# Setting the pad rows of the expert queues in nine stages during the front, in place of pads at the front's end

## The reference

```
x = layernorm(x + dilated_attention(x))           # 16 heads, segments of 64, every second token
x = layernorm(x + cross_attention(x, ctx))        # 16 heads, causal, keys and values from ctx
x = layernorm(x + moe(x))
# moe: probs = softmax(x @ gate_w); 8 of 32 experts for each token, weights renormalised
#      pairs are sorted by expert; an expert takes at most C = 1024 of them (2048*8/32*2), the rest are dropped
#      y = (silu(xg @ w_gate) * (xg @ w_up)) @ w_down ;  out[token] += weight * y
```

## Time and profile before

| | us |
|---|---|
| median of 3 runs | 622.81 (622.03 to 623.3) |
| the profiled execution | 623.45 |
| its span, first to last instruction | 621.8 |
| PE busy | 512.0 (82%) |
| DVE busy | 367.2 (59%) |
| ACT busy | 335.4 (54%) |
| POOL busy | 399.8 (64%) |

### The profile page before, as it was taken

How to read it: one execution, slowest core, us unless ns; L and a number is a source line. 1 busy time by engine, 2 the same in 40 slices (tenths; PEclk the granted TensorE clock), 3 DMA queues, 4 the chain that set the end, 5 groups by cost and what they waited for, 6 DMA issues and landing times.

```text
span 621.8 us, 17381 instructions
## 1 busy us (share of the span) xinstructions
PE 512.0 (82%) x5065; PEld 393.7 (63%) x5066; DVE 367.2 (59%) x1527; ACT 335.4 (54%) x1204; POOL 399.8 (64%) x604
## 2 busy tenths in 40 slices
PE   2888998888888888885119999999999999994994
PEld 2555555555555555542008888888888888883773
DVE  1468787777777787763304555555555555552664
ACT  2266666666666666663005666666666666661112
POOL 6553666666666666556715777777777768774653
PEclk9599999999999999996558999999999999996998
DMA  9999999932222222222785656656655556666994
GB/s 196 281 242 311 343 341 338 337 135 84 74 74 84 74 79 80 77 85 90 260 272 164 183 177 180 185 171 189 188 180 176 179 171 186 186 180 249 427 418 153
DMA packets 82301, 121.30 MB, mean 195 GB/s; under 512 B 13011, under 2 KB 71901, under 8 KB 80224
## 3 DMA queue, kind: packets, MB, share of 16 engines
q1 hardware_dynamic: 64896, 79.51, 42.0%
q0 software_dynamic: 14016, 38.44, 17.4%
q10 hardware_dynamic: 3360, 2.98, 1.5%
HBM read 56.07 MB, written 69.01 MB: 201 GB/s over the span
## 4 chain that ended last, share of the span: by engine, by line
PE 42%; POOL 16%; issue 14%; DVE 12%; DMA 6%; ACT 5%; ACTq 3%; POOLq 1%; SPq 1%; DVEq 0%
PE bank L796 16%; PE bank L812 11%; POOL queues L533 10%; PE bank L788 7%; DMA wall<-results 4%; DVE kP L1048 3%; ACT pr L873 3%; PE bank L806 3%; ACTq L297 2%; POOL rz L498 1%; POOL rz L492 1%; POOL pair_z L569 1%; DVE nmax L1025 1%; PE bank L614 1%; PE bank L604 1%
## 5 line engine op out<-in xcount | busy, mean ns | idle before, releaser
L559 POOL DMA_INDIRECT results<-ys,wcol x152 | 150.2, 988 | 26.2 <-POOL pscrap L548 24.1
L533 POOL DMA_INDIRECT queues<-x,xidx x128 | 128.5, 1004 | 37.2 <-issue 36.3
L796 PE MATMUL bank<-wall,xtT 128*128 x616 | 127.0, 329 | 0.1
L873 ACT ACTIVATE pr<-bank,nmax 128x128 f32<-128x128 f32 x256 | 90.9, 370 | 29.1 <-DVE nmax L1025 29.1
L796 PEld LDWEIGHTS bank<-wall,xtT 128*128 128x128 f32 x616 | 98.5, 194 | 0.5 <-issue 0.5
L966 ACT ACTIVATE ys<-bank,wcol 128x256 f32<-128x256 f32 x152 | 72.1, 474 | 44.5 <-PE bank L812 44.5
L1219 DVE SCALAR_TENSOR_TENSOR tg<-th,bank 128x96 f32<-128x96 f32 x154 | 39.1, 254 | 90.8 <-ACT th L960 90.6
L788 PE MATMUL bank<-ident,xt 128*128 128x128 f32 x310 | 63.4, 286 | 34.2 <-DMA xt<-queues 22.9
L812 PE MATMUL bank<-wall,hT 96*128 x304 | 90.8, 380 | 0.0
L788 PEld LDWEIGHTS bank<-ident,xt 128*128 128x128 f32 x310 | 59.2, 198 | 48.7 <-DMA xt<-queues 23.9
L604 PE MATMUL bank<-kP,qS 128*128 128x512 f32 x128 | 67.1, 606 | 0.0
(11 more groups left out here) (178 smaller groups left out, 879.6 us busy)
## 6 DMA issues: line engine op xcount, KB each, us to landing
xt<-queues SPq DMA_DIRECT2D x162, 160.0 KB, 2.2
results<-zeros SPq DMA_DIRECT2D x16, 1024.0 KB
wall<-results SPq DMA_DIRECT2D x16, 1024.0 KB, 13.9
queues<-zeros SPq DMA_DIRECT2D x32, 160.0 KB, 2.8
wall<-in_L_ffn_w_gate SPq DMA_DIRECT2D x4, 768.0 KB, 11.5
wall<-in_L_ffn_w_up SPq DMA_DIRECT2D x4, 768.0 KB, 13.6
wall<-in_L_ffn_w_down SPq DMA_DIRECT2D x4, 768.0 KB, 13.0
results<-ys,wcol POOLq DMA_INDIRECT x152, 2.6
```

Of the source, the lines that this page charges most:

```text
L533: pool.indirect_dma_start(xg, bass.IndirectOffsetOnAxis(ap=xidx[:, par, k:k + 1], axis=0), x2[:, par, :], None, bounds_check=last_row, oob ...
L559: pool.indirect_dma_start(yr, bass.IndirectOffsetOnAxis(ap=wcol[:, u, 1:2], axis=0), ys[:, u, :], None, bounds_check=last_y, oob_is_err=Fa ...
L796: ins = pe.matmul(bank[2 + u % 2][:, 0:2 * INTER].rearrange("p (g i) -> p g i", g=2), xtT[:, u % 2, kk, :], wall[:, bass.ds(e, GU)].rearrange(
L873: ins = act.activation(pr[:, g % 2, q, :], pS[g % 2][:, q * P:(q + 1) * P], ACT.Exp, bias=nmax[:, 4 * g + q:4 * g + q + 1], accum_out=den[ ...
```

## The change

SP no longer sets results right after the weight loads. It works through 16 stages, one DMA each, and waits for each before the next (semaphore `cleared`). Stage s, for s from 0 to 8 (QT is 8), sets rows s*128 to s*128+127 of all 32 queues to the pad row, in one DMA of 128 x 32 rows. Stages 9 to 15 each set one 1 MB block of `results` (blocks 0 to 6). Then come the 18 idle blocks and the other nine blocks of `results` (7 to 15, semaphore `yr_zero`), with no waits between them. POOL waits in the front for stage r ahead of tile r's copy and scatters. The pads at the front's end go with their waits on SP, ACT and POOL, and with them `tab_p`, `eoff` (one copy on POOL) and the matmul that counted for `tab_p`.

```diff
-        def pad_queues(eng, engine, first, last, signal):
-            for e0 in range(first, last, 8):
-                rows = neighbours(engine, tab_p[0:1, e0:min(e0 + 8, last)], NE * STRIDE - P)
-                for r in rows:
-                    eng.dma_start(xg[bass.ds(r, P), :], zeros[:, :]).then_inc(signal, 16)
...
             sp.wait_ge(consts, N_CONST)
+            queues_v = xg[0:NE * STRIDE, :].rearrange("(e s p) w -> s p e w", e=NE, p=P)
+
+            def clear_results(b, signal):
+
+                r = b * P * TOPK
+                sp.dma_start(yr[r:r + P * TOPK, :].rearrange("(p k) d -> p k d", k=TOPK),
+                             zeros[:, 0:D].unsqueeze(1).to_broadcast([P, TOPK, D])).then_inc(signal, 16)
+
+            for s in range(NB):
+                if s <= QT:
+                    sp.dma_start(queues_v[s], zeros[:, :].unsqueeze(1).to_broadcast([P, NE, XW])).then_inc(cleared, 16)
+                else:
+                    clear_results(s - QT - 1, cleared)
+                sp.wait_ge(cleared, 16 * (s + 1))
             for k in range(IDLE):
                 r = NE * STRIDE + k * P
                 sp.dma_start(xg[r:r + P, :], zeros[:, :]).then_inc(idle_zero, 16)
-            for b in range(NB):
...
-            sp.wait_ge(dveH.sem, dveH.at(0, "tp"))
-            pad_queues(sp, ET.SP, 0, PADS[0], pad_zero)
+            for b in range(NB - QT - 1, NB):
+                clear_results(b, yr_zero)
+
             sp.wait_ge(dveH.sem, dveH.at(0, "tx"))
...
             for k in range(2):
                 sp.wait_ge(scattered[k], 16 * TOPK * NB // 2)
-            sp.wait_ge(pad_zero, 16 * PADS[1])
-            sp.wait_ge(pad_late, 16 * (NE - PADS[1]))
             sp.wait_ge(idle_zero, 16 * IDLE)
...
-                put(pool.tensor_copy, eoff[:, :], eoff_i[:, :])
...
                     pool.wait_ge(dveR.sem, dveR.at(r, "idx"))
+                    pool.wait_ge(cleared, 16 * (r + 1))
                     if not last:
                         keep(r, par)
...
             three_stages(pool, step, lambda: None)
 
-            pool.wait_ge(dveH.sem, dveH.at(0, "tp"))
-            pad_queues(pool, ET.Pool, PADS[1], NE, pad_late)
             keep(NB - 1, (NB - 1) % 2)
...
             pool.wait_ge(dveH.sem, dveH.at(0, "tx"))
-            pool.wait_ge(yr_zero, 16 * NB)
+            pool.wait_ge(yr_zero, 16 * (QT + 1))
...
                 pe.wait_ge(actB.sem, actB.at(NB - 1, "T3"))
-                pe.matmul(pW[0:1, 96:96 + NE], onesb[:, 0:1], seen[:, :], start=True, stop=True)
...
-            act.wait_ge(dveH.sem, dveH.at(0, "tp"))
-            pad_queues(act, ET.Activation, PADS[0], PADS[1], pad_zero)
...
-                dve.tensor_tensor(tab_p[0:1, :], pW[0:1, 96:96 + NE], eoff[0:1, :], ALU.add).then_inc(s, 1)
```

More of the change, by code:

```diff
@@ L37 @@
 YB = 10
-PADS = (14, 28)
 LAST = (4, 4, 4, 2, 2)
@@ L46 @@
 B_CONST = FIRST_CONST + 23
-N_CONST = 54
+N_CONST = 53
 assert MAXB % UN == 0
@@ L118, in build @@
         eoff_i = sb("eoff_i", [P, NE], I32)
-        eoff = sb("eoff", [P, NE])
         ufar = sb("ufar", [P, NE])
@@ L192, in build @@
         tab_x = sb("tab_x", [1, TAB + 2 * LEAD], I32)
-        tab_p = sb("tab_p", [1, NE], I32)
         tab_n = sb("tab_n", [1, 1], I32)
@@ L237, in build @@
         peH = Steps(sem("peH"), "count place table")
-        dveH = Steps(sem("dveH"), "took tp nblk nblkb skipb cum past n n2 fe fx tg tw tx")
+        dveH = Steps(sem("dveH"), "took nblk nblkb skipb cum past n n2 fe fx tg tw tx")
         peF = {n: sem(f"peF_{n}") for n in ("xT", "gu", "hT", "y")}
@@ L252, in build @@
         idle_zero = sem("idle_zero")
-        pad_zero = sem("pad_zero")
-        pad_late = sem("pad_late")
+        cleared = sem("cleared")
         yr_zero = sem("yr_zero")
@@ L331, in _ @@
                 sp.dma_start(xg[r:r + P, :], zeros[:, :]).then_inc(idle_zero, 16)
-            for b in range(NB):
-                r = b * P * TOPK
-                sp.dma_start(yr[r:r + P * TOPK, :].rearrange("(p k) d -> p k d", k=TOPK),
-                             zeros[:, 0:D].unsqueeze(1).to_broadcast([P, TOPK, D])).then_inc(yr_zero, 16)
-            sp.wait_ge(dveH.sem, dveH.at(0, "tp"))
-            pad_queues(sp, ET.SP, 0, PADS[0], pad_zero)
+            for b in range(NB - QT - 1, NB):
+                clear_results(b, yr_zero)
             sp.wait_ge(dveH.sem, dveH.at(0, "tx"))
```

## The result

| | before | changed |
|---|---|---|
| median of the runs, us | 622.54 (4 runs, 622.03 to 623.3) | 654.45 (4 runs, 653.46 to 657.74) |
| ratio | | 1.0507 (95% interval 1.0475 to 1.0539) |
| the profiled execution | 623.45 | 653.46 |
| its span | 621.8 | 651.7 |

A forecast was written before the change was run, and what follows sets the result against it. The loop through POOL was taken to bound the front, with zeroing stages pacing it after the change. 623.45 + 44 lateness - 9.9 pads = 657.5, less 0.6 is 656.9, taken as 656; range 640 to 680.

The forecast's parts named there:

- The loop through POOL: Front: next tile's reciprocal root stands behind this tile's scatters on POOL, so holding POOL holds the front; step 16.5 us.
- What goes, 9.9 us: Front's end: without pads, first block load follows the last scatter's landing, 9.9 us sooner; bounds 9 to 10.5.
- Start of stage 0, end at 68.2: SP's first stage: issued at 47.72 behind weight loads, done at 68.2; front 8.6 us late at its first scatter.
- Period 20.9: Stages 1 to 8: 19.05 us of bytes at 344 GB/s plus the dry gap, against 16.5; tile 8 44 us late.
- After stage 8: Stages 9 to 15 take 5.9 us each; remaining zeros end near 325, hidden before the last scatter at 353; lateness stays 44.
- The clock, cost nothing: PE in stages 0 to 8: clock falls to 0.50 in stalls, hidden by the stage; costed at nothing, 16 us without cover.
- B: Rival, full rate: stages stream like 8 KB rows, period 17.2, +2.4 us, 625, including everything up to 638; chance 0.10.
- C: Rival, faster: clears keep up with the front, period 15.4, only stage 0's 6.7 us remain, 619.6; chance 0.04.
- the rule of the Trainium skill: Stage with scatters: 2.0 us + bytes/436 GB/s per DMA gives 17.0 us, change near level; weighed against 344 GB/s from the trace.
- D: Rival, slow writes: rows spread over 32 queues write slower; 718 at 253 GB/s, 682 at 300; chance 0.10.
- E: Rival, clock: PE at 0.50 for most of each step makes the loop 23.3 us, 19 us more, 675; chance 0.06.

The follow-up runs named there:

- run with eight stages and both orders: Changed kernel with stages and seven results blocks ahead of expert weights, two stages in flight, stage 8 replaced by a results block: 612.17 us, ratio 0.9812 against the kernel before.

## Why the prediction was right

*The loop through POOL.* Right: nine tiles in a row wait for the stages, the rest of the front follows them, and its own step behind the gate is still 16.4 to 16.5. The run with eight stages and both orders shows that taking the gate's lateness away gives all of it back.

*What goes, 9.9 us.* Measured 10.1 in the profile and 9.8 (ratios 1.0664 and 1.0507) when the pads were kept. The last scatter landed 2.5 after its start, and the first block load went 2.7 after it, 2.9 forecast; the 2.6 borrowed from the results' scatters was good.

*Start of stage 0, end at 68.2.* Measured 68.3. SP issued it at 46.64, not 47.72, and the rate for zeros alone came out at 376, not 369.

*Period 20.9.* Measured (231.38 - 68.36)/8 = 20.4. The two parts were each a little too high: 18.7 to 18.8 for the bytes (350 GB/s; 19.05 at 344 forecast) and 1.5 for the drain (1.9 forecast), by the run with two stages in flight. Over eight stages this is the 4 us by which the lateness, 44 forecast, was 39.8. It is nearly all the error of the sum in this profile: 657.5 by the sum, 653.5 measured. The prediction allowed up to 0.5 us a stage for scatters that move in the dry gap, 4 in all, and took 0.9; the whole allowance would have met the profile. Whether the drain is short for that reason no run tells apart.

*After stage 8.* The cover held, with more to spare: SP was through with issuing at 303.5, the first block load at 351. Stages 9 to 15 took 4.8 each, not 5.9. What the prediction did not see is that traffic which ends late went with a loss of 2.9 and 4.6 us at the front's last scatters before it was itself the last thing waited for; in the changed kernel it ended early enough, in two of the experiments not.

*The clock, cost nothing.* Right for the changed kernel: the granted clock was 0.87 on average from 66 to 231, and the period stayed the stage's. But the cover is the gate. In the profile of the run with the pads kept the low clock reached into the first free step, and that step was 2.4 us longer. The changed kernel's runs spread over 4.3 us, those of before over 1.3; that this is where the spread comes from is only argued.

*The rivals.* B and C asked for a stage to go at the rate of 8 KB rows. It went at 350. By the rule of the Trainium skill weighed in the prediction (DMA: Bandwidth & Descriptors, section Anatomy of one DMA — SWDGE (gpsimd) path), which is stated for DMAs of GpSimd's path, a stage is estimated at 17.0. Applied to SP's stages, the trace agrees with neither its slope for these rows (350 GB/s) nor, quite, its fixed part, 2.0 there and a drain of 1.5 here. D asked for slow writes to 32 queues: 376 GB/s says no. E asked for POOL to wait for VectorE, with a loop of 23.3. In the changed kernel it waited for the zeros at all nine tiles, and with two stages in flight the front kept a period of 18.8, so the loop itself takes no longer than that.

## What to carry to other kernels

A wait put into a loop costs (its supply's period less the loop's own) for every turn that it gates, so compare the two periods first: bytes over the rate of the nearest rows of the same size, with all that shares the engines, plus the drain if each transfer is waited for alone. Before giving up on such a change, look at what stands ahead of the supply in its queue and at how many are in flight: here the order of one queue and a second semaphore turned +32 us into -10 (ratio 0.9842), and with one stage fewer into -12. And free DMA time is only free where it ends ahead of the next burst of small transfers that someone waits for.

## What the runs showed of the hardware that was not expected

- Rows of 1280 B written to 32 places 1.47 MB apart went at 376 GB/s from 54 to 66 us, no slower than neighbouring blocks of them had (369). It is not one figure: in the run with the stages ahead of the weights they went at 337 from 38 to 52, with no scatter of rows beside them. Why, no run settles.
- To wait for one stage before the next is issued cost 1.5 us of a loaded stream, less than the 2.2 us that a small load takes to land. One more serial step of 0.16 MB cost 1.6, its own bytes included.
- The scatters of the last two tiles, 16 of them, stand in a row on POOL. The second of them waits 2.1 to 2.5 us without other traffic and 5.1 with it. What it waits for the profile gives only as "issue".
